# A graph network of two layers: last turn's one-hots moved, a mean left out, keys through PSUM, one wait's condition

## The reference

```python
def _L0_gnn_ref(node_feat, edge_feat, eps, src, dst):
    m = jax.nn.relu(node_feat[src] + edge_feat)
    neigh = jax.ops.segment_sum(m, dst, num_segments=node_feat.shape[0])
    return (1.0 + eps[0]) * node_feat + neigh
def _L1_gnn_ref(node_f, src, dst):
    ...
    x = node_f * jax.lax.rsqrt(out_deg)[:, None]
    agg = jax.ops.segment_sum(x[src], dst, num_segments=n)
    return agg * jax.lax.rsqrt(in_deg)[:, None]
x = _layernorm(x + _L0_gnn_ref(x, edge_attr_32, L0_gnn_eps, src, dst), axis=-1)
x = _layernorm(x + _L1_gnn_ref(x, src, dst), axis=-1)
```

## Time and profile before

| what | us |
|---|---|
| median of three runs (5188.18 to 5191.56) | 5188.48 |
| the profiled execution | 5192.55 |
| its span, first to last instruction | 5190.4 |
| PE / DVE / ACT / POOL busy in it | 3318.3 / 3288.3 / 2750.1 / 2966.5 |

### The profile page before, as it was taken

The page is one execution under the profiler, slowest core; times in us unless marked ns, Lnnn a source line. Parts: engine busy times, 40 slices in busy tenths (PEclk is TensorE's granted clock), DMA queues, the critical chain, the costliest instruction groups (busy, mean ns, idle before and its releaser), DMA issues. The chain is left out here.

```text
span 5190.4 us, 62756 instructions
## 1 busy us (share of the span) xinstructions
PE 3318.3 (64%) x21148; PEld 1678.6 (32%) x21148; DVE 3288.3 (63%) x4729; ACT 2750.1 (53%) x2907; POOL 2966.5 (57%) x3134
## 2 busy tenths in 40 slices
PE   4555555555555555555555555555555999999997
PEld 1111111111111111111111111111113888888886
DVE  7766666666666666666666666666666444444445
ACT  4555555555555555555555555555553555555553
POOL 7777777777777777777777777777772000000000
PEclk7666666666666666666666666666666999999998
DMA  3333333333333333333333333333335999999995
GB/s 125 120 119 136 126 119 119 120 126 128 131 123 119 119 119 119 131 131 119 119 120 124 124 136 123 119 119 119 119 128 179 326 325 323 326 324 325 325 325 206
DMA packets 269133, 867.70 MB, mean 167 GB/s; under 512 B 90218, under 2 KB 140218, under 8 KB 252602
## 3 DMA queue, kind: packets, MB, share of 16 engines
q1 hardware_dynamic: 169107, 815.98, 42.3%
q0 software_dynamic: 100000, 51.40, 5.3%
HBM read 486.77 MB, written 380.38 MB: 167 GB/s over the span
## 5 line engine op out<-in xcount | busy, mean ns | idle before, releaser
L166 POOL DMA_INDIRECT rows<-in_x,src_t x3125 | 2964.8, 949 | 959.5 <-issue 946.1
L688 PE MATMUL built<-x_parts,b_hot 100*128 100x490 bf16 x3000 | 1292.6, 534 | 1758.3 <-ACT big L622 1743.2
L622 ACT ACTIVATE big<-built 128x980 bf16<-128x980 f32 x1500 | 1805.0, 1229 | 546.2 <-PE built L688 542.9
L688 PEld LDWEIGHTS built<-x_parts,b_hot 100*128 100x128 bf16 x3000 | 249.9, 111 | 2647.8 <-ACT big L622 2029.4
L1061 PE MATMUL applied<-counts,x_parts 128*96 128x160 bf16 x12250 | 916.1, 233 | 17.5 <-DVE x_parts L873 17.5
L427 DVE TENSOR_TENSOR sum_ps<-sum_ps,rows 128x416 f32<-128x416 f32 x250 | 143.0, 572 | 1229.9 <-DMA rows<-in_x,src_t 1224.7
L668 PE MATMUL agg<-hot,msg 128*128 128x512 bf16 x3125 | 903.2, 440 | 4.9 <-DVE msg L457 4.9
L1061 PEld LDWEIGHTS applied<-counts,x_parts 128*96 128x96 bf16 x12250 | 880.2, 123 | 80.7 <-issue 18.8
L146 DVE TENSOR_TENSOR x_parts<-iota_ps,hk_g 100x3920 bf16<-100x3920 f16 x375 | 819.5, 2185 | 0.0
L1017 ACT ACTIVATE counts<-built 128x980 bf16<-128x980 f32 x496 | 594.3, 1239 | 387.5 <-PE built L1044 387.5
L146 DVE TENSOR_TENSOR hot<-iota_ps,s_hi 128x5252 bf16<-128x5252 f16 x250 | 691.4, 2766 | 0.0
(11 more groups left out here) (135 smaller groups left out, 1445.4 us busy)
## 6 DMA issues: line engine op xcount, KB each, us to landing
stash<-big SPq DMA_DIRECT2D x125, 2940.0 KB
counts<-stash SPq DMA_DIRECT2D x250, 1470.0 KB, 8.7
rows<-in_x,src_t POOLq DMA_INDIRECT x3125
edge_t<-in_edge_attr SPq DMA_DIRECT2D x61, 800.0 KB
big<-in_dst SPq DMA_DIRECT2D x1, 1562.5 KB
big<-in_src SPq DMA_DIRECT2D x1, 1562.5 KB
src_t<-in_src SPq DMA_DIRECT2D x61, 24.8 KB
dst_t<-in_dst SPq DMA_DIRECT2D x61, 24.8 KB
```

The lines of the kernel that those rows point to most:

```text
L166: gp.indirect_dma_start(rows_d[:, j, :], None, nodes, bass.IndirectOffsetOnAxis(ap=src_d[:, j:j + 1].bitcast(U32), axis=0),).then_inc(s, 16)
L622: sc.activation(stage[:, slot % 2, q, :, d0:d0 + 2 * SPAN].rearrange("p c (b d) -> p b c d", b=2), built[n % 2][:, :, 0:KEYS].rearrange("p ...
L688: last = te.matmul(built[n % 2][:, b, 0:KEYS], b_hot[:, r, t, :], key_hot[:, r, t, :], start=True, stop=True)
```

## The change

Four edits. (1) In the last turn with rows (g = G) DVE's order is another: indices, the sums of the turn before and all one-hots but lo_hot(0) stand ahead of the first add, which waits for the rows. (2) The end no longer takes the mean off: the sum y + x_n is squared as it is, and ACT's order becomes squares, squares, deviation, deviation. (x_n is the result of a layer norm, and sums of its rows are added to it, so the mean of a row is zero but for rounding.) (3) In the preparation the firsts are copied into PSUM as well and subtracted from there, and the keys are made in three passes instead of two, with what lies between in PSUM, five pieces of the 32 columns to a pass (LOWS). (4) GpSimd's condition reads `g >= 8` instead of `g >= 5`.

```diff
+                def lows(bank, n):
+                    return bank[0:NC, 0:n * TP].rearrange("g (j p) -> g j p", p=TP)
+                first_ps = sum_bank[0:NC, 512 - JT:512]
+                LOWS = [(0, 10, lows(built[0][:, :, :].rearrange("p b k -> p (b k)"), 10)),
+                        (10, 10, lows(built[1][:, :, :].rearrange("p b k -> p (b k)"), 10)),
+                        (20, 5, lows(agg_bank, 5)), (25, 5, lows(fold_bank, 5)), (30, JT - 30, lows(sum_bank, JT - 30))]
...
-                    after(ve.tensor_copy(c_first[:, :], c_dst[:, :, 0]))
+                    V(ve.tensor_copy(c_first[:, :], c_dst[:, :, 0]))
                     n_first = V.n
-                    V(ve.tensor_tensor(c_rel, c_dst, last_dim(c_first[:, :], TP), ALU.subtract))
+                    after(ve.tensor_copy(first_ps, c_dst[:, :, 0]))
+                    V(ve.tensor_tensor(c_rel, c_dst, last_dim(first_ps, TP), ALU.subtract))
...
-                    after(ve.scalar_tensor_tensor(c_key, c_hi, -float(C), c_src, ALU.mult, ALU.add))
-                    after(ve.scalar_tensor_tensor(c_key, c_key, float(SPAN), c_rel, ALU.mult, ALU.add))
+                    for t, n, lo in LOWS:
+                        V(ve.tensor_scalar(lo, c_hi[:, t:t + n, :], -float(C), None, ALU.mult))
+                    ve.wait_ge(s_v, V.n)
+                    for t, n, lo in LOWS:
+                        V(ve.tensor_tensor(lo, lo, c_src[:, t:t + n, :], ALU.add))
+                    ve.wait_ge(s_v, V.n)
+                    for t, n, lo in LOWS:
+                        V(ve.scalar_tensor_tensor(c_key[:, t:t + n, :], lo, float(SPAN), c_rel[:, t:t + n, :], ALU.mult, ALU.add))
...
+                            if isinstance(g, int) and g == G:
+
+                                ve.wait_ge(z_part2[1], g - 1)
+                                indices()
+                                sums_out()
+                                ve.wait_ge(z_idx[3], g)
+                                dst_hot(0)
+                                hi_hot(0)
+                                hi_hot(1)
+                                dst_hot(1)
+                                lo_hot(1)
                                 add(0)
...
-                                if not isinstance(g, int) or g >= 5:
+                                if not isinstance(g, int) or g >= 8:
...
                         for k in range(CUT):
                             normed(k)
-                        mean(0)
-                        normed(CUT)
-                        centred(0)
-                        for k in range(CUT + 1, len(FR)):
+                        summed(0)
+                        for k in range(CUT, len(FR)):
                             normed(k)
+                        summed(1)
                         variance(0)
-                        mean(1)
                         result(0)
-                        centred(1)
                         variance(1)
                         result(1)
```

More of the change, by code:

```diff
@@ L300, in layer_0 @@
                 taken = sb("taken", [R, WD])
-                sum_ps = pb("sum_ps")[:, 0:JA * D].rearrange("p (j d) -> p j d", d=D)
+                sum_bank = pb("sum_ps")
+                sum_ps = sum_bank[:, 0:JA * D].rearrange("p (j d) -> p j d", d=D)
                 built = [own.enter_context(nc.psum_tensor(f"built{k}", [P, 2, 512], F32)) for k in range(2)]
@@ L464, in step, with sums_out @@
                                 chunk(0, 0, 0)
-                            if sends(g):
+                            def sums_out():
+                                ve.wait_ge(z_agg, g - 1)
+                                ve.tensor_tensor(degree[:, :], degree[:, :], agg_degree, ALU.add)
+                                ve.tensor_copy(taken[:, :], agg).then_inc(z_taken, 1)
+                            if isinstance(g, int) and g == G:
[8 more added lines that the diff above has]
+                                lo_hot(1)
                                 add(0)
-                            if builds(g):
-                                chunk(g, k, 1)
-                            if sends(g):
                                 left(0)
-                                indices()
-                            if isinstance(g, int) and g == G:
                                 for k in range(2):
@@ L475, in step @@
                                 ve.memset(x_0[P - 32:P, TAIL:C, :], 0.0).then_inc(z_clear, 1)
[L476 to L482, removed]
                                 last_part(0)
-                                ve.wait_ge(z_idx[3], g)
-                                dst_hot(0)
+                                lo_hot(0).then_inc(z_hot, 1)
                                 add(1)
-                                hi_hot(0)
                                 left(1)
[L491 to L494, removed]
                                 last_part(1)
+                            else:
+                                if sends(g):
+                                    add(0)
+                                if builds(g):
+                                    chunk(g, k, 1)
+                                if sends(g):
+                                    left(0)
+                                    indices()
+                                if adds(g):
+                                    sums_out()
+                                if builds(g):
+                                    chunk(g, k, 2)
+                                if sends(g):
+                                    last_part(0)
+                                    ve.wait_ge(z_idx[3], g)
+                                    dst_hot(0)
+                                    add(1)
+                                    hi_hot(0)
+                                    left(1)
+                                    lo_hot(0).then_inc(z_hot, 1)
+                                    hi_hot(1)
+                                    lo_hot(1)
+                                    dst_hot(1)
+                                    last_part(1)
                             if adds(g):
@@ L1211, in finish_1 @@
                 sq = sb("sq1", [P, C, D])
-                stat = sb("stat1", [P, C])
                 var = sb("var1", [P, C])
@@ L1242, in normed, with summed @@
                                              wide(r_in, c0, c0 + n), ALU.mult).then_inc(h_used, 1)
-                        def mean(h):
+                        def summed(h):
                             c0, c1 = PART[h]
                             ve.wait_ge(h_used, (CUT, len(FR))[h])
[L1247 to L1256, removed]
+                            ve.tensor_tensor(y[:, c0:c1, :], y[:, c0:c1, :], x_n[:, c0:c1, :], ALU.add).then_inc(h_summed, 1)
                         def variance(h):
@@ L1285, in _, with squares, deviation @@
                     def _(sc):
-                        for h, (c0, c1) in enumerate(PART):
-                            sc.wait_ge(h_centred, h + 1)
+                        def squares(h):
+                            c0, c1 = PART[h]
+                            sc.wait_ge(h_summed, h + 1)
                             sc.activation(sq[:, c0:c1, :], y[:, c0:c1, :], ACT.Square).then_inc(h_squares, 1)
+                        def deviation(h):
+                            c0, c1 = PART[h]
                             sc.wait_ge(h_var, h + 1)
                             sc.activation(rstd[:, c0:c1], var[:, c0:c1], ACT.Sqrt, bias=ln_eps[:, 0:1], scale=1.0 / D).then_inc(h_dev, 1)
+                        squares(0)
+                        squares(1)
+                        deviation(0)
+                        deviation(1)
                     @block.sync
```

3 lines of the change are left out of this document (1 added, 2 removed).

## The result

The changed kernel takes 5179.58 us (median of 20 runs, 5176.76 to 5181.78), the kernel before 5188.48 (20 runs, 5186.44 to 5191.56): a ratio of 0.9982 with a 95% interval of 0.9976 to 0.9989, so 8.9 us less. 5180.1 was predicted, inside 5175.5 to 5185.0, and "within 0.2%" was the likeliest case. The profiled execution took 5176.98 us, with a span of 5174.9.

The account below looks back on a forecast made before the run. The prediction took GpSimd's gathers to bound the first layer from about 148 us and PE the second. Keys +4.3, last turn -4.9 and end -7.8 made -8.4 us, from 5188.48 to 5180.1 us, range 5175.5 to 5185.0.

Parts of the forecast that it names:

- The bound: First layer from about 148 us: GpSimd's gathers set the pace, 25 gathers or 31.25 us a turn.
- the gate: GpSimd's wait ahead of group 4's first gather, opened by PE's third-turn sums; predicted to move from 147.68 to 152.0 us.
- The keys, +4.3: Preparation on DVE: three passes of 3.80 us instead of two make keys, gate and every later gather 4.3 us later.
- Rival 1: Keys' first pass runs at two elements a cycle, so keys come only 2.7 us later: 5178.5 us; chance 0.10.
- Nothing gives the 4.3 us back: First three turns, between keys and group 4: the keys' 4.3 us delay reaches the gate in full.
- all four long gathers: Preparation: gathers of 3.14, 3.73, 3.92 and 3.23 us, held by DVE; three become usual, lifting 7.4 us from GpSimd.
- The lead that GpSimd gains, 0: Ahead of group 4: GpSimd arrives 7.4 us earlier but waits 7.4 us longer; the condition's edit changes nothing.
- rival 2: Group 4: the loop's entry makes the wait, not PE's sums, so GpSimd keeps 7.4 us: 5168.4 us; chance 0.05.
- The last turn, -4.9: Behind the last rows: one-hots done ahead of them let PE start its last 25 products 4.9 us earlier.
- The end, -7.8: Behind the last transposes: without statistics and centring the last product ends at 5178.4 instead of 5186.22, 7.8 us earlier.
- rival 3: Keys' passes: PSUM is dear in place; at 3.2 ns an element the kernel takes 5200.9 us; chance 0.03.
- Rival 4: Last turn: the one-hots don't fit ahead of the rows, losing up to the whole 4.9 us: 5185.0; chance 0.06.

Follow-up runs that it names:

- e5: The changed kernel with eight turns written out ahead of the loop instead of four, GpSimd's wait for the sums kept from group 4 on: 5838.53 us, ratio 0.9995.
- e2: The kernel before with only the change's order of the last turn: 5840.85 us, ratio 1.0003 to the kernel before on the same chip.

## Why the prediction was right

*The bound.* From the gate to the last gather the layer is GpSimd's, in both traces, at one gather per 1.25 us. But the pace is not the same: 3024 steps take 3775.7 us after and 3780.6 before, so the last gather starts 2.4 us earlier than before, where 4.3 later was predicted. These 4.9 us are in no term. A gather is busy 945.3 ns before and 943.5 after, which makes 5.4 us. They don't go with the change: from 300 to 3900 us a gather takes 945.2 before and 943.6 after, but 945.5 in e5, which has all of the change, and 943.2 in e2, which has only the last turn. So two profiled executions can lie some 5 us apart by this alone. With +2.6, -5.7 and -7.8 the 4.9 us make up the difference of the two profiled executions, 15.6 us, to 0.3 us. The medians differ by 8.9 only: the profiled execution of before lies 4.1 us above its median, the one of after 2.6 below.

*The keys, +4.3: the mechanism was right, the size at the gate 2.6.* The passes take 3.8 us each, and the keys are 4.35 us later (49.14 against 44.79). Rival 1, the first pass at two a cycle, falls: its piece of 1000 takes as long as the others'. "Nothing gives the 4.3 us back" was wrong. Turn 1's sums end 3.4 us later than before, turn 2's 2.8, turn 3's 2.5. These are before's (the third is in the earlier trace rows):

```profile
96.15 4.81 PE L668 MATMUL agg<-hot,msg 128*128 128x512 bf16 x19
...
119.78 4.94 PE L668 MATMUL agg<-hot,msg 128*128 128x512 bf16 x19
```

The 19 products take 4.81 and 4.94 us there, 4.26 and 4.68 after: more of them ran at the higher clock (granted clock in these four stretches 0.89 and 0.86 before, 1.00 and 0.91 after). That is 0.8 of the 1.8 us given back. Another 0.4 came back ahead of base_all (61.42 against 57.51, 3.9 later), the rest in small steps. The prediction had allowed 1 to 2 us for the clock's phase in these turns, but left it out of the term.

The page "SBUF — State Buffer" of the Trainium skill, "Who interferes with whom", says that an operation with both inputs in SBUF contends only with GpSimd's reads, and infers that writing descriptors isn't hindered. The prediction had taken the page's rule on descriptors for all four long gathers, but by this section it speaks only for the one beside L351 and L352, which do two elements a cycle; beside L344, L353 and L354 none would have been held by it. The rows differ: beside L353 and L354 gathers take 3.92 and 3.23 us, beside passes with one operand in PSUM 0.94; the measurement decides. A gather also reads its indices, src_t, from SBUF, and no run here tells whether that read or the writing was held.

*The lead that GpSimd gains, 0.* Right: the wait grew from 3.37 to 13.77 us, and the condition's edit did nothing, since the wait stands ahead of group 4. That it is a wait for sums was shown by e5, and at 5188 us by the gather's start, 0.80 us behind the third sums' end before and 0.82 after. By rival 2 the gather would have started 7.4 us earlier than before, at 140.3 us; it started at 150.24.

*The last turn, -4.9: 5.7 measured*, from the last gather's start to the last sums (14.40 us where it was 20.07). Of the 0.8 us more, 0.95 come from the sums of the turn before, which ended 5.4 us ahead of the last gather and not 4.4 (their 19 products took 4.26 us, not 4.79, and began 0.4 us earlier against the gathers), so that DVE was 0.2 us late for the rows and not 1.15; the 25 products took 0.13 longer. The load of x_0 cost nothing: from the last sums to the end's last transposes are 1219.2 us, before 1219.0.

*The end, -7.8: 7.8 measured*, twice.

*The sum* of the terms as measured, +2.6 - 5.7 - 7.8, is -10.9, and -8.9 [-12.5, -5.7] by the medians. The predicted -8.4 lies inside; it had the keys 1.7 us too dear and the last turn 0.8 too small. Those two misses add up to 2.5 us, so that the forecast comes within half a microsecond of the median is luck; that it lies inside the range is not.

*The rivals.* Rivals 1 and 2 fall by the rows above; rival 3 too, since no pass is dear: 3.80 us were worked out from the copy's row, and 3.77 to 3.80 measured. Rival 4, the one-hots that don't fit, fell at 5188 us (DVE 0.2 us late); on the slower chips its outcome came true, by stalls that it had not named.

## What to carry to other kernels

Before you free an engine, ask who it waits for next: the 7.8 us that GpSimd gained became 10.4 us more of waiting, and the passes that gave them lay on the chain that opens the gate. At 5188 us one-hots moved into the wait for the last rows, and statistics dropped from a serial end, paid about what their rows said. And a cover that is short by 0.2 us on one chip was gone on four others: time both kernels on more than one chip before you trust it.

## What the hardware did that I had not expected

On the four chips of the experiments the kernel before takes 648 to 675 us longer. The changed kernel has a trace of both kinds, and its span is 667 us longer: 93 up to the gate, 565 from there to the last gather, 12 from it to the last sums, and nothing (-2) behind. The period of a group is about 36 us and not 31.25, since GpSimd waits some 5 us in each of 120 turns for something that the trace doesn't name (the waits of the changed kernel there):

```profile
POOL rows L166 <- remote: 602.3, 120, 5.4
```

The other engines are held too, and by more. ACT's copies of the keys, which follow one another within 0.35 us at 5188 us, in the changed kernel there:

```profile
50.94 0.59 ACT L624 ACTIVATE hk_all<-built 100x500 f16<-100x500 f32 x1 [0.25 <-PE built L399]
53.86 0.59 ACT L624 ACTIVATE hk_all<-built 100x500 f16<-100x500 f32 x1 [2.33 <-PE built L399]
61.54 0.59 ACT L624 ACTIVATE hk_all<-built 100x500 f16<-100x500 f32 x1 [7.10 <-remote]
...
81.84 0.59 ACT L624 ACTIVATE hk_all<-built 100x500 f16<-100x500 f32 x1 [10.62 <-remote]
...
126.64 0.59 ACT L624 ACTIVATE hk_all<-built 100x500 f16<-100x500 f32 x1 [10.61 <-remote]
...
151.64 0.59 ACT L624 ACTIVATE hk_all<-built 100x500 f16<-100x500 f32 x1 [0.25 <-PE built L399]
```

They come every 11.2 us until GpSimd stops at 136.6, and at their old pace soon after. The old keys, 4.0 us earlier, meet this with most of their copies made: in the kernel with the end alone 14 of the 16 are through by 64 us, and base_all stands at 98.3 us (106.5 with the last turn too), not at 153.4. So on one chip the old keys are 51.5 us ahead at base_all (98.3 and 149.8 us, the kernels with the end and with the keys alone), and on another 46.9 (106.5 and 153.4); at the gate 11.1 and 10.1 us of it are left. The changed kernel needs 89.4 us from base_all to the gate here and 88.8 at 5188 us: GpSimd stands still by then and nothing is held. The kernel with the end alone needs 128.9, since its first turns run beside gathers until 143 us. The second layer, which has no gathers, takes as long as ever. What it is that holds the engines (a hand-over between them, their code, a queue) no run here shows. Nor does one tell the chip from the occasion: the 5188 us come from one set of runs, and all later ones, on four chips, took longer. So it stays open why the same program behaves otherwise there.
